# A four-layer graph attention kernel: GpSimd waits in the middle of each pair's gathers for an expansion of scores on TensorE

## The chip, the cores and the metric

The kernel runs on one core of a Trainium2 chip. What is measured is the device time of one execution in microseconds. The engines of the core are TensorE (PE in the profile; PEld is its weight load), VectorE (DVE), ScalarE (ACT), GpSimd (POOL) and SyncE (SP); they run their own instruction streams and are kept in order by counting semaphores, here called counts: an instruction raises a count when it is done, and another engine waits until the count has reached a number.

## What is computed

Four graph attention layers over N = 4096 nodes with 256 features, four heads of 64 (one head in layer 1), each applied to a layer-normed and rectified input and added to the residual. The graph is given as a dense 0/1 matrix `adj` that has some nine neighbours per node. Layer 0, cut to what matters (layers 1 and 2 have the same form with other slopes and ends; layer 3 is scaled dot-product attention over the transposed mask):

```python
h = jnp.maximum(_layernorm(x), 0.0)
Wh = (h @ W).reshape(n, heads, d)
s_i = jnp.einsum('nhd,hd->nh', Wh, a[:, :d])
s_j = jnp.einsum('nhd,hd->nh', Wh, a[:, d:])
e = leaky_relu(s_i[:, None, :] + s_j[None, :, :])
e = jnp.where((adj == 0)[:, :, None], -jnp.inf, e)
alpha = softmax(e, axis=1)
x = x + elu(jnp.einsum('ijh,jhd->ihd', alpha, Wh))
```

## The kernel before

**Sparse work on a dense input.** The kernel reads `adj` once (the first 240 us), turns it into lists of edges, and from then on works edge by edge. A second, dense program in the same kernel is for inputs that don't fit the lists; it doesn't run here. The nodes are cut into T = 32 tiles of 128. Each tile has its edges laid out over KT = 9 columns of 128 partitions, one edge for each partition and column.

**Gathers.** For each tile and column one indirect DMA, issued by GpSimd at L810, fetches the table row of each edge's neighbour (256 features and its score terms) from `tab_d` in DRAM into the buffer `gb`. So a tile has 9 gathers, and a pair of tiles 18. `gb` is a ring: in layers 0 to 2 it has room for RING = 8 tiles. `gp_gather` (L801) waits before tile t for the count `agg` of tile t - 8, that is, until TensorE has summed up the tile whose place is taken; with that it runs four pairs ahead of the arithmetic. At the start of a layer it first waits for the layer's table, then issues the first 8 tiles without a wait. Nothing else is in GpSimd's stream in the layers.

**The groups.** Work goes by groups n = 0 to 16: a group is a pair of tiles (2n, 2n + 1) up to n = 14, and a single tile in the last two. `pe_layer`, `act_layer` and `vec_layer` run one step for each group, in an order that is written out by hand, and the layer that follows (l = L.n + 1) is prepared inside the same steps: as soon as a tile of x is final, its norm, hidden values, projection and table row for the next layer are made.

TensorE's step n (`pe_step`, L1966) is: tile 2n and tile 2n + 1 (`pe_tile`, L1995: nine accumulating matmuls each, shown as 18 records at L1925, count `agg` at the end of each tile); `pe_turn` for group n + 1 (L1901, count `turned_raw`); `pe_hidden`, the transposes of the next layer's hidden values (L1830, count `turned`); the first projection (L1851 and lines after it, count `projected`); `pe_turn_back` (L1909, count `back`); the second projection; in layer 2 also `pe_q` (L1865); and last `pe_expand` for group n + 2 (L1875, 18 matmuls, count `expanded`), which spreads each node's score term over its edges.

VectorE's step n (`vec_step`, L1701) is: multiply the gathered rows of group n by their weights (`vec_weigh`, L1609, six of them, count `weighed`); scores of group n + 1 from the expansion and the gathered terms (`vec_scores`, L1498 to L1518, waits for `expanded`, count `raw_ok`); finish the group's tiles (`vec_finish`, L1620 to L1643); two scans over the scores for the maximum of each node (`vec_shift`, L1554 and L1556, count `shifted`); subtract it (`vec_less`, L1566, waits for `back`, count `lessened`); and statistics and score terms of the next layer.

ScalarE's step (`act_step`, L1076) makes for each tile the matrix that sums edges into nodes (`act_distance` L1008 and `act_equal` L1015, count `S_ok`; L1008 waits for `agg`), scales the outputs (L1047), copies transposes and projections out of PSUM (L926, count `hT_ok`; L948, L959 or L962, count `tabbed`), sends the table rows to DRAM (L966) and exponentiates the scores (`act_exp`, L1024, count `p_ok`).

`expanded` rises by one for each group, 17 in a layer.

Of the kernel before, what the change touches and what calls it, by code (L numbers as in the profile page):

```python
# [445 lines left out]
class Sparse:  # L446
# [354 lines left out]
    def gp_gather(self, e, L, t):  # L801
        gb, s = self.rows(L, t), t % L.ring
        if L.n == 0:
            e.wait_ge(self.listed, t // 4 + 1)
            if t == 6:
                e.wait_ge(self.seg_in, 16 * HS)
        if t >= L.ring:
            e.wait_ge(self.agg, T * L.n + t - L.ring + 1)
        for k in range(KT):
            e.indirect_dma_start(gb[:, 0, k, 0:L.row], None, self.tab_d[L.n],  # L810
                                 bass.IndirectOffsetOnAxis(ap=self.idx[:, t, k:k + 1], axis=0)).then_inc(self.gat[s], 16)
# [1346 lines left out]
```

## Time and profile before

| | us |
|---|---|
| median of 3 runs | 2522.17 |
| lowest and highest of them | 2516.67 and 2530.95 |
| span of the profiled execution | 2533.3 |
| GpSimd busy in it | 1126.0 (44%) |
| VectorE busy in it | 1446.1 (57%) |
| TensorE busy in it | 1404.5 (55%) |
| ScalarE busy in it | 1221.3 (48%) |

The profiled execution is one run of the program under the hardware profiler. Times in the rows below are in us from the span's start. By the gathers, layer 0 goes from 269.9 to about 840, layer 1 to about 1367, layer 2 to about 1914, and layer 3 to the end.

### The profile page before, as it was taken

What the parts mean: (1) busy time and instruction counts of PE and PEld (TensorE: products, weight loads), DVE (VectorE), ACT (ScalarE), POOL (GpSimd) and SP (SyncE); (2) the same over time, 40 slices, a digit from 0 to 9 for tenths busy, and PEclk for the clock granted to TensorE, in tenths of its full rate; (3) what the DMA queues carried; (4) which work ended last, traced back from release to release, by engine and by line L of the source; (5) the groups of instructions that cost most, each with busy time, mean ns of one, the idle gap of its engine ahead of it and who ended that gap; (6) DMA issues with size and microseconds to landing.
All of it is one profiled execution on the core that took longest, in us unless ns stands there. A gap on an engine that the chain in (4) does not pass through costs nothing.

```text
span 2533.3 us, 25363 instructions
## 1 busy us (share of the span) xinstructions
PE 1404.5 (55%) x7265; PEld 1001.1 (40%) x7265; DVE 1446.1 (57%) x4007; ACT 1221.3 (48%) x2974; POOL 1126.0 (44%) x1172
## 2 busy tenths in 40 slices
PE   3564214556657216657674347666694456556655
PEld 2432113444445204445452124444452345444544
DVE  3788656556567315555664145555582566666666
ACT  6775314666667204445563045555582243444344
POOL 0000525666550566656613755555505344455441
PEclk9965556677777656777776567888897677777778
DMA  9993313344430334434412433444415445555451
GB/s 359 388 373 96 75 41 98 105 109 115 99 96 22 93 95 108 112 100 107 108 42 75 106 103 111 111 111 111 110 60 185 119 142 152 148 175 147 143 151 57
DMA packets 163550, 320.34 MB, mean 126 GB/s; under 512 B 31562, under 2 KB 80464, under 8 KB 163408
## 3 DMA queue, kind: packets, MB, share of 16 engines
q0 software_dynamic: 64512, 191.91, 28.3%
q1 hardware_dynamic: 81200, 105.63, 12.6%
q10 hardware_dynamic: 17696, 21.12, 2.4%
q8 instruction: 61, 1.00, 0.2%
q14 instruction: 81, 0.66, 0.1%
HBM read 288.74 MB, written 29.84 MB: 126 GB/s over the span
## 4 chain that ended last, share of the span: by engine, by line
PE 28%; issue 25%; DVE 21%; another core or an unknown queue 16%; ACT 7%; DMA 2%; SPq 1%; ACTq 0%; POOL 0%; DVEq 0%; POOLq 0%
PE ps L1925 17%; PE ps L1851 5%; DVE s_gb L1609 4%; DVE s_sc L1541 2%; ACT s_a L842 2%; DVE s_F L1554 2%; DMA s_adj<-in_adj_dram 2%; PE ps L1889 1%; DVE s_F L1556 1%; DVE s_ST L1417 1%; ACT s_S L1008 1%; PE ps L1865 1%; DVE s_tmp L1537 1%; SPq L642 1%
## 5 line engine op out<-in xcount | busy, mean ns | idle before, releaser
L810 POOL DMA_INDIRECT s_gb<-s_tab,s_ji x1152 | 1121.4, 973 | 1107.1 <-PE ps L1925 368.1
L1925 PE MATMUL ps<-s_gb,s_S 128*128 128x264 f32 (+1 forms) x2304 | 688.5, 457 | 331.3 <-issue 261.1
L1925 PEld LDWEIGHTS ps<-s_gb,s_S 128*128 128x128 f32 x2304 | 523.3, 231 | 480.2 <-issue 318.7
L1008 ACT ACTIVATE s_S<-s_count,s_ji 128x128 f32<-128x128 f32 x1152 | 352.8, 390 | 333.7 <-remote 197.3
L1609 DVE TENSOR_TENSOR s_gb<-s_gb,ps 128x768 f32<-128x768 f32 x384 | 341.7, 948 | 7.7 <-ACT ps L1024 5.9
L1851 PE MATMUL ps<-s_wx,s_hT 128*128 128x264 f32 (+2 forms) x512 | 237.3, 602 | 157.0 <-issue 66.2
L1015 ACT ACTIVATE s_S<-s_S,s_ones 128x384 f32<-128x384 f32 x384 | 209.6, 603 | 86.1 <-remote 67.3
L1851 PEld LDWEIGHTS ps<-s_wx,s_hT 128*128 128x128 f32 x512 | 117.9, 255 | 215.8 <-issue 148.8
L1498 DVE TENSOR_REDUCE s_sx<-ps 128x144 f32<-128x432 f32 (+3 forms) x68 | 30.3, 446 | 245.1 <-remote 242.2
L1889 PE MATMUL ps<-s_early,s_rows_of 128*128 128x256 f32 x416 | 129.9, 466 | 63.1 <-issue 42.9
L1537 DVE TENSOR_TENSOR s_tmp<-ps,s_gb 128x512 f32<-128x512 f32 (+1 forms) x160 | 98.5, 632 | 106.0 <-issue 45.9
L1620 DVE TENSOR_SCALAR s_rc<-ps,s_alone 128x4 f32<-128x4 f32 (+1 forms) x128 | 28.2, 220 | 225.4 <-PE ps L1925 107.8
L1909 PE MATMUL ps<-s_ident,s_F 32*128 32x32 f32 (+3 forms) x272 | 34.1, 246 | 211.0 <-issue 144.3
L1554 DVE TENSOR_TENSOR_SCAN s_F<-s_d,ps 32x512 f32<-32x512 bf16 (+3 forms) x68 | 81.8, 1202 | 113.0 <-remote 64.0
L1889 PEld LDWEIGHTS ps<-s_early,s_rows_of 128*128 128x128 f32 x416 | 95.0, 234 | 83.6 <-issue 45.7
L1024 ACT ACTIVATE ps<-s_sc 128x72 f32<-128x72 f32 (+3 forms) x68 | 15.0, 220 | 231.6 <-DVE s_sc L1567 124.4
L842 ACT ACTIVATE s_a<-s_adj 128x4096 fp8e4<-128x4096 int32 x32 | 115.4, 3606 | 15.6 <-DMA s_adj<-in_adj_dram 15.6
L1909 PEld LDWEIGHTS ps<-s_ident,s_F 32*128 32x128 f32 (+3 forms) x272 | 27.7, 167 | 236.5 <-issue 155.8
L790 POOL IOTA s_u<- 128x1152 f32 x1 | 1.4, 1399 | 236.5 <-DVE s_flag_t L1410 236.5
L1901 PE MATMUL ps<-s_ident,s_sc 128*32 128x128 f32 (+3 forms) x272 | 44.2, 282 | 111.5 <-issue 78.7
L1541 DVE TENSOR_REDUCE s_sc<-s_tmp 128x8 f32<-128x512 f32 (+1 forms) x160 | 97.1, 624 | 0.0
L1566 DVE TENSOR_TENSOR s_sc<-s_sc,ps 128x24 f32<-128x24 f32 (+3 forms) x136 | 23.0, 170 | 128.1 <-remote 99.3
(206 smaller groups left out, 2007.2 us busy)
## 6 DMA issues: line engine op xcount, KB each, us to landing
s_adj<-in_adj_dram SPq DMA_DIRECT2D x32, 2048.0 KB, 16.1
s_gb<-s_tab,s_ji POOLq DMA_INDIRECT x1152
s_mine<-s_tab SPq DMA_DIRECT2D x128, 128.0 KB
s_tab<-s_tb ACTq DMA_DIRECT2D x32, 256.0 KB
s_tab<-s_tb ACTq DMA_DIRECT2D x31, 260.0 KB
s_xs<-in_x_dram SPq DMA_DIRECT2D x8, 512.0 KB, 16.4
s_early<-s_q SPq DMA_DIRECT2D x32, 128.0 KB
s_tab<-s_tb ACTq DMA_DIRECT2D x15, 257.0 KB
```

The costliest lines, as they stand in the source:

```text
L810: e.indirect_dma_start(gb[:, 0, k, 0:L.row], None, self.tab_d[L.n], bass.IndirectOffsetOnAxis(ap=self.idx[:, t, k:k + 1], axis=0)).then_in ...
L842: e.activation(self.a8[:, q % 2], self.adj[:, r], ACT.Copy, saturate=False).then_inc(self.conv)
L1008: m = e.activation(self.s_part(U)[:, i, :], self.count[:], ACT.Square, bias=self.irel[:, t, k:k + 1], scale=-1.0)
L1015: e.activation(self.s_part(U), self.s_part(U), ACT.Relu, bias=self.ones[:, 0:1], scale=-4.0).then_inc(self.S_ok)
L1537: e.tensor_tensor(part(x), self.bank((0, 6, 7)[x % 3]).rearrange("p (k d) -> p k d", k=2)[:, 0:2 if c < 4 else 1], g4[:, 0, 2 * c:min(2 * ...
L1541: e.tensor_reduce(sc[:, 2 * c - 2:min(2 * c, KT), :], part(x - 1).rearrange("p k (h d) -> p k h d", h=4), AX, ALU.add).then_inc(self.dotted)
L1554: e.tensor_tensor_scan(F, d0[:, 0:HE], pc, SEG, ALU.add, ALU.max).then_inc(self.v)
L1609: e.tensor_tensor(vv[:, k], vv[:, k], wide(p[:, k, :], 3, L.hd), ALU.mult).then_inc(self.weighed)
L1851: x = e.matmul(o, self.hT[:, j, k, :], self.wx[:, k, a:b], start=(k == 0), stop=(k == 1 and l < 2))
L1889: m = e.matmul(self.bank((0, 6, 7)[x % 3], D * i, D), self.unfolding(t, k, k + 1), self.q[:, t % 2, :], start=True, stop=True)
L1909: m = e.transpose(pt[:, rows * k:rows * (k + 1)], F[:, P * k:P * k + P], self.ident[0:rows, 0:rows])
L1925: m = e.matmul(o, S[:, i, :], g4[:, 0, k, lo:lo + D + 2 * L.heads], start=(k == 0), stop=(k == KT - 1))
```

## The change

Two lines are added to `gp_gather`. They apply to layers 0 to 2 and to the second tile of each pair that is gathered under the ring's wait, t = 9, 11, ... 29. Before the nine gathers of such a tile GpSimd waits until `expanded` has reached 17 L.n + t // 2 - 1, which is the number it has once the expansion of group t // 2 - 2 is done. The pair that is being gathered is group t // 2. TensorE makes that expansion at the end of step t // 2 - 4, the step in which it also sums tile t - 8.

```diff
         if t >= L.ring:
             e.wait_ge(self.agg, T * L.n + t - L.ring + 1)
+        if L.n < 3 and t >= L.ring and t % 2 and t < 30:
+            e.wait_ge(self.expanded, 17 * L.n + t // 2 - 1)
         for k in range(KT):
             e.indirect_dma_start(gb[:, 0, k, 0:L.row], None, self.tab_d[L.n],
```

Nothing else is changed: the DMAs, their number and their order on the queue are the same, and so are the streams of the other engines.

## Rows read from the trace of the kernel before

**Rows 1.** Page, costliest groups: line, engine, operation, count; busy, mean; idle before, releaser.
```profile
L810 POOL DMA_INDIRECT s_gb<-s_tab,s_ji x1152 | 1121.4, 973 | 1107.1 <-PE ps L1925 368.1
```

**Rows 2.** Windows (columns in the first row): a pair of layer 0, of layer 2, without gathers.
```profile
core 0: us, PE busy (x) PEld busy (x) DVE busy (x) ACT busy (x) POOL busy (x), PEclk, DMA share, GB/s
610.87:637.85 26.98, 16.57 (x75) 12.27 (x74) 16.60 (x47) 17.48 (x50) 17.33 (x19) 0.78 0.43 110
1617.80:1648.65 30.85, 19.77 (x87) 12.86 (x86) 16.45 (x44) 16.23 (x44) 17.27 (x18) 0.83 0.43 113
779.57:800.17 20.60, 15.17 (x66) 11.78 (x65) 16.31 (x48) 17.03 (x49) 0.00 (x0) 0.75 0.04 14
```

**Rows 3.** Timeline, GpSimd: start, length, engine, line [idle before, releaser]; after 18 gathers each.
```profile
637.85 0.94 POOL L810 DMA_INDIRECT s_gb<-s_tab,s_ji  x1 [4.47 <-remote]
...
970.50 0.95 POOL L810 DMA_INDIRECT s_gb<-s_tab,s_ji  x1 [3.28 <-remote]
```

**Rows 4.** Timeline, layer 0, late part of a run of gathers.
```profile
622.25 0.68 PE L1875 MATMUL ps<-s_si,s_ST 128*128 128x24 bf16 x18
...
624.28 6.77 PE L1925 MATMUL ps<-s_gb,s_S 128*128 128x264 f32 x18 [1.35 <-issue]
...
635.33 0.38 PE L1925 MATMUL ps<-s_gb,s_S 128*128 128x264 f32 x1 [1.41 <-issue]
...
636.75 5.22 PE L1925 MATMUL ps<-s_gb,s_S 128*128 128x264 f32 x16 [1.03 <-issue]
636.95 0.61 DVE L1498 TENSOR_REDUCE s_sx<-ps 128x144 f32<-128x432 f32 x1 [8.14 <-remote]
637.13 2.73 ACT L1008 ACTIVATE s_S<-s_count,s_ji 128x128 f32<-128x128 f32 x9 [3.68 <-remote]
```

**Rows 5.** Timeline, layer 0 after its last gather.
```profile
786.39 0.38 DVE L1498 TENSOR_REDUCE s_sx<-ps 128x72 f32<-128x216 f32 x1
```

**Rows 6.** Timeline, layer 0, after the run of gathers that begins at 637.85.
```profile
642.24 0.60 PE L1830 MATMUL ps<-s_ident,s_tb 128*128 128x128 f32 x4
643.09 0.58 ACT L926 ACTIVATE s_hT<-ps 128x512 f32<-128x512 f32 x1
...
645.78 0.43 PE L1909 MATMUL ps<-s_ident,s_F 32*128 32x32 f32 x4 [0.93 <-DVE s_F L1556]
...
647.37 2.06 PE L1851 MATMUL ps<-s_wx,s_hT 128*128 128x258 f32 x4 [1.15 <-ACT s_tb L960]
...
649.22 0.68 PE L1875 MATMUL ps<-s_si,s_ST 128*128 128x24 bf16 x18
...
650.33 0.18 DVE L1566 TENSOR_TENSOR s_sc<-s_sc,ps 128x24 f32<-128x24 f32 x1 [3.37 <-remote]
...
658.84 0.38 ACT L959 ACTIVATE s_tmp<-ps 128x256 f32<-128x256 f32 x1 [4.49 <-remote]
```

**Rows 7.** Timeline, layer 2: an expansion, and the next start of gathers.
```profile
1632.63 0.61 PE L1875 MATMUL ps<-s_si,s_ST 128*128 128x24 bf16 x18
...
1648.65 0.95 POOL L810 DMA_INDIRECT s_gb<-s_tab,s_ji  x1 [8.41 <-PE ps L1925]
```

**Rows 8.** Timeline, layer 1: the first gather after the layer's first 72.
```profile
944.23 0.94 POOL L810 DMA_INDIRECT s_gb<-s_tab,s_ji  x1 [10.71 <-remote]
```

**Rows 9.** Timeline, TensorE in layer 0, beside 27 gathers from 420.1 to 454.9.
```profile
426.74 0.61 PE L1875 MATMUL ps<-s_si,s_ST 128*128 128x24 bf16 x18
430.81 10.24 PE L1925 MATMUL ps<-s_gb,s_S 128*128 128x264 f32 x36 [3.46 <-DVE s_gb L1609]
...
441.32 0.60 PE L1830 MATMUL ps<-s_ident,s_tb 128*128 128x128 f32 x4
459.72 2.09 PE L1851 MATMUL ps<-s_wx,s_hT 128*128 128x258 f32 x4 [17.80 <-ACT s_hT L926]
...
465.21 0.68 PE L1875 MATMUL ps<-s_si,s_ST 128*128 128x24 bf16 x18
```

**Rows 10.** Timeline, GpSimd in layer 1: two run starts, one after the other.
```profile
1078.90 0.95 POOL L810 DMA_INDIRECT s_gb<-s_tab,s_ji  x1 [6.13 <-PE ps L1925]
...
1113.61 0.95 POOL L810 DMA_INDIRECT s_gb<-s_tab,s_ji  x1 [12.20 <-PE ps L1925]
```

## The prediction

> **What bounds the kernel now.** I read four views, in this order. First the groups of instructions: GpSimd's 1152 gathers take 949 to 973 ns each and one starts every 1.25 us [rows 1], so the 18 gathers of a pair (two tiles of 128 nodes) need 22.6 us. Then the windows: a pair of layer 0 takes 27.0 us, one of layer 2 30.9 us, and a pair without any gather beside it 20.6 us [rows 2]. No engine is busy for more than 20 us in any of them. So neither the gathers alone nor the arithmetic alone sets the pair's time; something between them does.
>
> The timeline of GpSimd shows the rhythm: 18 gathers without a break, then a pause of 4.5 or 3.3 us that ends with a count from TensorE (`agg`, the end of the first tile of a pair) [rows 3]. The timeline of the other engines shows the something. TensorE finishes an expansion at 622.9; VectorE, which has nothing else to do for 8.1 us, reads that count only at 636.95, 14.0 us later. TensorE's next tile ends at 631.05, and ScalarE (and GpSimd) act on it at 637.13, 6.1 us later; TensorE itself issues its next matmuls singly, with 1.4 us idle before one, until 636.75 [rows 4]. All of it comes free at once, 3.3 to 3.8 us after the last gather (633.4). Where no gathers run, the same count is there when VectorE comes for it, with no idle time at all [rows 5]. I call the time in which counts are held **the clog**. Counts from TensorE that are raised up to about 7 us into a run of gathers go through (turned 642.84, used 643.09). The `back` raised at 646.2, 8.4 us into the run, is used at 650.3, and the second `projected` (649.4) at 658.8 [rows 6]. So a run of 18 gathers has a clog from about +8 to +26 us, counted from its first gather.
>
> What matters is therefore **what lies in the clog**. Now a run starts when tile A of a pair is summed (in the rows: expansion 622.25, tile A 624.28, run 637.85). Tile B (4 us) and the chain that goes back and forth between TensorE and the others (transposes, `turned`, hT, projection, row, second projection, expansion, at +12.1 us) lie in the clear part. The clogged part holds the next tile A, a stream of 18 matmuls that needs few counts. That is a good alignment.
>
> **The change, part by part.** It removes nothing and adds 33 waits (odd tiles 9 to 29, three layers). No DMA, no arithmetic. The wait itself is an instruction of some 20 to 50 ns on GpSimd; 33 of them I cost at nothing. What is queued behind it on GpSimd is the pair's second 9 gathers and all later ones; who waits for those is VectorE's scores, six tiles later, so a late gather costs nothing directly. SP's and ScalarE's queues are passed by nothing. What changes is when the gathers run, and so where the clog falls.
>
> Step 1, the first pause. The first 9 gathers end at +11.3 us. The expansion waited for is finished at +12.1 (637.85 to 649.9) in layer 0 and at +15.4 in layer 2 (1617.8 to 1633.2) [rows 6, 7]. The clog after 9 gathers must first drain. No row shows such a drain alone: 18 gathers have pauses of 3.3 to 4.5 us and 72 of them 10.7 us [rows 3, 8], 0.12 to 0.14 us for each gather, so 9 have 2 to 3 us, of which 0.7 us is GpSimd's own restart; below by the 0.8 us of the expansion itself. I take 2.3, near the rows with the short pauses. The second half then starts at about +13.6 (layer 0) or +16.1 (layer 2).
>
> Step 2, whether there is a second pause. Tile A of the next pair starts 1.4 to 2 us after the expansion and takes 6.8 us [rows 4], so its count is raised 7 to 8 us after the second half began: at the very edge where counts still go through. The second half ends only at +11.3 after its start. If the count is in by then, GpSimd goes on without a pause, and its run of 18 now starts at the expansion, not at the end of tile A.
>
> Step 3, what that does. From the expansion, tiles A and B take 10.2 us [rows 9] and their transposes end near +13, deep in the clog of the run. The chain can then not go on before the run ends and drains: 0.7 + 22.6 + 3.6 = 26.9 us, and from `turned` to the end of the expansion it takes 7.1 us (642.84 to 649.9) [rows 6]. A pair takes 34.0 us. And GpSimd waits for that same expansion, so the next run starts there again: the bad alignment keeps itself. The trace of before has it once, where 27 gathers ran without a stop: TensorE was through with both tiles and transposes at 441.9 and got its next work at 459.7, 17.8 us idle, and from expansion to expansion went 38.5 us [rows 9]. A second case is in layer 1, where tile B came late in its run: 34.7 us for that pair [rows 10].
>
> The sum, against 2533.3 us of the profiled execution. Layer 0: 34.0 - 27.0 = 7.0 us a pair. Layer 2: its chain is 3.3 us longer (+15.4 against +12.1), so 37.3 - 30.9 = 6.4. Layer 1: about 33 (its chain is a little shorter than layer 0's; the row with 34.7 bounds it from above, the present 28.6, five runs from 970.50 to 1113.61, from below), so 4.4 [rows 2, 3, 10]. Each layer has 11 such pairs. The bad alignment starts at once in layer 0 (the expansion that tile 11 will wait for ends at 465.9, 6 us after its gathers start now [rows 9]), but tile A's count is at the edge, so some pairs get a second pause instead and cost nothing. I take 8 pairs of 11 in layers 0 and 2, where tile A follows the expansion at once, and 3 of 11 in layer 1, where it follows later and so misses the edge more often: 8 x 7.0 + 3 x 4.4 + 8 x 6.4 = 120 us. 2533 + 120 = 2653 for a profiled execution. The median of the runs is 0.4% under the profiled one (2522.17 to 2533.3), so **2640 us**. With all 33 pairs: 77 + 48 + 70 = 195 us, 2717. Layer 3 and the first 380 us have no such wait and stay.
>
> **The rivals.** (a) *Two pauses a pair, faster.* If tile A's count is just late, more than 8 us into the second half, each half of 9 gathers gets its own drain and the clog is cut from 18 us a pair to about 2 x 5. A pair is then 2 x (11.3 + 2.3) = 27.2 us, the same as layer 0 has, 1.4 less than layer 1, and in layer 2, where the present pause of 8.4 us [rows 7] shows TensorE itself held by the clog, the expansion at 15.4 + 0.7 and then 13.6 make 29.7, 1.2 less: -15 - 13 = -28 us, 2494. With a drain of 2.6 us it is -10. For it: the clog is the only reason why a pair takes 27 and not 20.6, and this halves it. Against it: 1 us decides, and a long wait for an expansion always lands on the wrong side. It would be visible in pairs of 27 with two pauses each. If even more of layer 2's excess goes (to the 26.5 us at which one drained run of 18 can repeat) the sum is -70, 2452. (b) *The wait does nothing.* Should the count of the expansion be there at +12.1, GpSimd loses 1 us in the middle and has a shorter pause at the end, which is 3.3 us or more everywhere: 2522. The held count [rows 4] speaks against it. (c) *All pairs bad*, 2717, the end of my forecast's own case.
>
> The Trainium skill speaks for (b): "Advanced Engine Details and Errata", section DMA Bandwidth Details, puts the overhead of a semaphore increment on TRN2 at about one cycle. By that rule the expansion's count would be seen when it is raised, no run of gathers could hold it, and the change would give 2522. The 14.0 us in the trace disagrees, and where both differ the trace decides.
>
> **How the numbers follow.** Forecast, run realigned to the expansion: 0.63, of which most lies in 2570 to 2720. Rival (a): 0.25, 2450 to 2510. Rival (b), or gains and losses that cancel: 0.12. A measurement of this kernel can tell about 0.5% (13 us) from no change. So faster 0.25, same 0.12, slower 0.63. The range has to reach (a) and the case of all pairs bad: 2490 to 2725 leaves out about 0.2. The forecast's own range is 2570 to 2725.
>
> **What would show it.** Right: in the changed kernel GpSimd pauses 8 to 11 us in the middle of a pair and not between pairs, from expansion to expansion goes 33 to 37 us, and TensorE sits idle some 12 us before the first projection of a pair, waiting for hT. Step 1 alone is right if the first 9 gathers are followed by 2 to 3 us. Step 2 is wrong if a pair has two pauses of 2 to 3 us each; then (a) holds. Step 3 is wrong if the pause is in the middle only and the pair still takes 27: counts would then pass through the clog that I take for held. If VectorE reads the expansion's count without idle time and nothing else moves, it is (b). The prediction fails above all if tile A's count comes 1 us later than I reckon.

## The result, and the profile after

The changed kernel takes **2712.81 us** (median of 4 runs, 2701.56 to 2719.67), the kernel before 2523.2: a ratio of **1.073** (95% interval 1.068 to 1.078). The profiled execution spans 2705.1 us, 171.8 more than before. Forecast were 2640 us and a slower kernel; 2713 is nearly the upper end of the forecast's own case, which had all pairs bad at 2717.

The page, four of the costliest groups (columns as in [rows 1]). GpSimd now stands idle before gathers 185 us longer in all, and the expansion (L1877) ends 355 us of its idle time. TensorE's projection (L1853) waits 492 us for hT, which ScalarE copies at L928; before it was 98 us. ScalarE's copy itself waits 475 us, and VectorE's first step on a summed tile (L1622) 489 us, for a count whose source the profile can't name (remote):

```profile
L812 POOL DMA_INDIRECT s_gb<-s_tab,s_ji x1152 | 1108.6, 962 | 1292.0 <-PE ps L1877 354.8
...
L1853 PE MATMUL ps<-s_wx,s_hT 128*128 128x264 f32 (+2 forms) x512 | 281.0, 697 | 565.3 <-ACT s_hT L928 492.1
...
L1622 DVE TENSOR_SCALAR s_rc<-ps,s_alone 128x4 f32<-128x4 f32 (+1 forms) x128 | 28.0, 219 | 565.8 <-remote 488.9
L928 ACT ACTIVATE s_hT<-ps 128x512 f32<-128x512 f32 (+1 forms) x67 | 38.4, 573 | 500.2 <-remote 475.3
```

Windows of one pair of layers 0, 1 and 2, each from one resumed run of gathers to the next. They answer [rows 2]; the work per pair is the same, only the time is longer. The clock granted to TensorE is lower (0.65 for 0.78 in layer 0), but it is busy only 0.6 us longer in the pair (17.17 for 16.57), so the clock does not explain the 6 us:

```profile
core 0: us, PE busy (x) PEld busy (x) DVE busy (x) ACT busy (x) POOL busy (x), PEclk, DMA share, GB/s
625.70:659.00 33.30, 17.17 (x74) 13.11 (x74) 16.70 (x47) 17.45 (x50) 17.26 (x18) 0.65 0.34 90
1105.80:1140.50 34.70, 17.85 (x79) 13.14 (x79) 15.80 (x49) 14.04 (x36) 17.02 (x18) 0.65 0.32 87
1695.60:1733.00 37.40, 18.82 (x88) 12.00 (x87) 16.58 (x45) 16.50 (x45) 16.99 (x18) 0.77 0.33 94
```

GpSimd's timeline, layer 0. The pauses of 10.8 to 11 us are in the middle of a pair (they answer [rows 3]); between pairs, at 603.83, the idle time is 0.43 us, hardly more than the 0.3 before any gather:

```profile
603.83 0.94 POOL L812 DMA_INDIRECT s_gb<-s_tab,s_ji  x1 [0.43 <-issue]
...
625.73 1.21 POOL L812 DMA_INDIRECT s_gb<-s_tab,s_ji  x1 [10.95 <-PE ps L1877]
...
659.00 0.94 POOL L812 DMA_INDIRECT s_gb<-s_tab,s_ji  x1 [10.84 <-PE ps L1877]
```

TensorE and then, in the last line, ScalarE in the pair between those pauses:

```profile
624.27 0.68 PE L1877 MATMUL ps<-s_si,s_ST 128*128 128x24 bf16 x18
628.06 11.05 PE L1927 MATMUL ps<-s_gb,s_S 128*128 128x264 f32 x36 [3.12 <-DVE s_gb L1611]
...
639.39 0.60 PE L1832 MATMUL ps<-s_ident,s_tb 128*128 128x128 f32 x4
652.04 2.09 PE L1853 MATMUL ps<-s_wx,s_hT 128*128 128x258 f32 x4 [12.05 <-ACT s_hT L928]
...
657.54 0.68 PE L1877 MATMUL ps<-s_si,s_ST 128*128 128x24 bf16 x18
...
651.39 0.60 ACT L928 ACTIVATE s_hT<-ps 128x512 f32<-128x512 f32 x1 [10.53 <-remote]
```

The expansion ends at 624.95 and the 18 gathers run from 625.7 to 648.1. Both tiles and their transposes are through at 640. ScalarE sees the transposes' count at 651.39, 11.4 us after it was raised and 3.3 us after the last gather; then come 7 us of chain, and the expansion, finished at 658.2, lets GpSimd go on. That is the loop of step 3.

That the second nine gathers of a pair come later is not itself the cost. VectorE waits for gathered rows as long as before, 37.5 us in all and in two places (here its line among the waits: total, times, longest); before it was 37.6:

```profile
DVE s_sc L1508 <- DMA s_gb<-s_tab,s_ji: 37.5, 2, 19.8
```

Where the time went: the time from a layer's third expansion to its sixteenth (ends of L1875 or L1877 in TensorE's timeline) is 353, 362 and 389 us in layers 0 to 2 of before and 402, 423 and 460 of after, +50, +61 and +71. The starts of layers are within 1 us of what they were, and layer 3 is 10 us shorter.

### The profile page after: what moved, and what is told of

Read it like the earlier page. It is cut to its first block, busy times and chain, and to the rows that moved or that the text cites. A ratio compares the mean times of both kernels' runs of the same rounds, so it can differ in the third digit from the quotient of the medians.

```text
span 2705.1 us, 25385 instructions
## 1 busy us (share of the span) xinstructions
PE 1391.5 (51%) x7265; PEld 996.5 (37%) x7265; DVE 1444.9 (53%) x4007; ACT 1220.3 (45%) x2974; POOL 1113.2 (41%) x1172
## 4 chain that ended last, share of the span: by engine, by line
another core or an unknown queue 29%; DVE 23%; PE 18%; issue 15%; ACT 10%; DMA 2%; SPq 1%; ACTq 0%; DVEq 0%
PE ps L1927 8%; PE ps L1853 6%; DVE s_gb L1611 5%; ACT s_S L1010 3%; DVE s_sc L1543 2%; DVE s_F L1556 2%; ACT s_a L844 2%; DMA s_adj<-in_adj_dram 1%; DVE s_F L1558 1%; PE ps L1867 1%; SPq L642 1%; DVE s_ST L1419 1%; DVE s_tmp L1539 1%; PE ps L1891 1%
## 5 line engine op out<-in xcount | busy, mean ns | idle before, releaser
L812 POOL DMA_INDIRECT s_gb<-s_tab,s_ji x1152 | 1108.6, 962 | 1292.0 <-PE ps L1877 354.8
L1927 PE MATMUL ps<-s_gb,s_S 128*128 128x264 f32 (+1 forms) x2304 | 619.5, 431 | 136.8 <-issue 76.7
L1927 PEld LDWEIGHTS ps<-s_gb,s_S 128*128 128x128 f32 x2304 | 490.9, 216 | 246.3 <-issue 91.9
L1853 PE MATMUL ps<-s_wx,s_hT 128*128 128x264 f32 (+2 forms) x512 | 281.0, 697 | 565.3 <-ACT s_hT L928 492.1
L1853 PEld LDWEIGHTS ps<-s_wx,s_hT 128*128 128x128 f32 x512 | 136.6, 295 | 634.3 <-ACT s_hT L928 503.9
L1622 DVE TENSOR_SCALAR s_rc<-ps,s_alone 128x4 f32<-128x4 f32 (+1 forms) x128 | 28.0, 219 | 565.8 <-remote 488.9
L928 ACT ACTIVATE s_hT<-ps 128x512 f32<-128x512 f32 (+1 forms) x67 | 38.4, 573 | 500.2 <-remote 475.3
L1911 PEld LDWEIGHTS ps<-s_ident,s_F 32*128 32x128 f32 (+3 forms) x272 | 33.7, 194 | 212.0 <-issue 141.8
L1049 ACT ACTIVATE s_y<-ps,s_rc 128x64 f32<-128x64 f32 x384 | 87.1, 307 | 4.7 <-DVE ps L1645 4.6
```

Source lines behind the costliest of these rows:

```text
L1049: m = e.activation(y[:, L.hd * h:L.hd * h + L.hd], ov[:, L.hd * h:L.hd * h + L.hd], ACT.Copy, scale=self.rc[:, j, h:h + 1])
L1853: x = e.matmul(o, self.hT[:, j, k, :], self.wx[:, k, a:b], start=(k == 0), stop=(k == 1 and l < 2))
L1927: m = e.matmul(o, S[:, i, :], g4[:, 0, k, lo:lo + D + 2 * L.heads], start=(k == 0), stop=(k == KT - 1))
```

## Experiments

Theory, **held counts**: while gathers follow closely, counts that TensorE raises are held till a backlog is served, and the change costs only because it moves the chain into that stretch. The spacing is the time from the start of one gather to the start of the next. Main rivals: the late gathers or the wait cost by themselves; any gather in flight holds counts, at whatever spacing.

The kernel before was run beside each experiment. In four sessions it took 2505 to 2549 us, as in the session of the result (2523); in two others it took 2006 and 2007 us. The traces from sessions of the first kind show held counts, except those of experiment 5, whose session is known only by the time of the kernel before (2507 us) and by the sign given in the last section. The traces from the other two show none. I call these sessions **held** and **free**. Chips differ between sessions, but one chip number stands for sessions of both kinds, so whether it is the chip, its host or something that changes with time stays open. Ratios are only compared within a session.

**1. The wait on an older expansion, and three more kernels: a free session.** First the wait alone (the diff is against the changed kernel):

```
-            e.wait_ge(self.expanded, 17 * L.n + t // 2 - 1)
+            e.wait_ge(self.expanded, 17 * L.n + t // 2 - 2)
```

> The same 33 waits in the same places, but each for the expansion one pair earlier, which was done some 27 us before. If what costs is the phase between the gathers and TensorE's chain (my theory, the held counts), nothing happens: no pause in mid-pair, 27.0 us per pair in layer 0, 2517 to 2531 us, ratio 1.00. If the waiting instruction itself, or its place in GpSimd's queue, cost something (rival), 33 of them would carry part of the 190 us, and the time would be above 2540 us.

Measured: 2010.8 us, ratio 1.001 (0.9995 to 1.003). The same as before, but so was everything that ran beside it. Next, the changed kernel with a run of gathers that starts at tile B (again against the changed kernel):

```
         if t >= L.ring:
-            e.wait_ge(self.agg, T * L.n + t - L.ring + 1)
+            e.wait_ge(self.agg, T * L.n + t - L.ring + (2 if L.n < 3 and t % 2 == 0 and t < 30 else 1))
```

> The changed kernel with one more edit: the first nine gathers of a pair are started one tile later (at the end of tile B, not of tile A). The wait of the change stays, and all gathers come later than in the changed kernel by their own waits. Theory of the held counts: the run starts 7.7 us after the expansion, the next expansion is made 8 us into the run (layer 0) or 11 (layer 2), so that at worst a pause of 2.3 us after nine gathers is added to one of 3.3: 26 to 28 us per pair in layer 0, at most 31 in layer 2, 2440 to 2540 us. Rival (late rows: it costs that the second nine gathers wait at all, and that VectorE gets their rows later): nothing gets better than in the changed kernel, 2700 us or more.

Measured: 2009.2 us, ratio 1.001 (0.999 to 1.003). The last two have one memset after each gather, without and with the waits of the change:

```
         self.idle = sb("idle", [P, 32])
...
+            if T * L.n + t + k:
+                e.wait_ge(self.idled, KT * (T * L.n + t) + k)
+            e.memset(self.idle[:], 0.0).then_inc(self.idled)
```

> The kernel before with a small GpSimd memset (128x32, result unused) after each gather and no new wait. It should bring the spacing of the gathers from 1.25 us to about 1.43 (0.13 for the memset and some 0.05 for its issue). Theory: counts are held because gathers are issued faster than about one in 1.40 us, which is how fast a backlog of 18 and of 72 was seen to drain. Then no count is held: 18 gathers take 25.8 us, VectorE reads TensorE's counts within 0.1 us in mid-run, a pair takes 26 to 27.5 us in all three layers (now 27.0, 28.6, 30.9), and the kernel takes 2400 to 2470 us although GpSimd does more. Rival (any gather in flight holds counts, at whatever spacing): each pair is 3 us longer, 29 to 30 us in layer 0, 2580 us or more.

Measured: 2012.2 us, ratio 1.002 (1.000 to 1.004). The spacing did not rise to 1.43 us but to 1.26: the memset fits into the 0.3 us between two gathers.

> The changed kernel (with its 33 waits) with the same memset after each gather. Theory: with no held counts the expansion waited for is finished at about the end of the first nine gathers (12.9 us at the new spacing) and is seen at once, so the wait costs 0 to 2 us a pair: within 60 us of the kernel with the memset alone, and below 2530 us. Rival (the wait costs because rows come late, whatever the counts do): 170 to 190 us above the kernel with the memset alone, with a pause in mid-pair of 10 us or more.

Measured: 2010.4 us, ratio 1.001 (0.999 to 1.003), against 2012.2 without the waits. So the 33 waits alone cost nothing in a free session, where they are always met before GpSimd comes to them (see below): the cost that I gave the instruction is right.

The trace of the first of the four shows what a session without held counts looks like. Here are two lines of its page: GpSimd's group among the costliest, and the gathers among the DMA issues, where the last number is the time to landing in us:

```profile
L812 POOL DMA_INDIRECT s_gb<-s_tab,s_ji x1152 | 1132.4, 983 | 572.9 <-issue 344.2
...
s_gb<-s_tab,s_ji POOLq DMA_INDIRECT x1152, 3.3
```

A window from the end of one expansion of layer 0 to that of the next (columns as above):

```profile
493.16:513.80 20.64, 15.40 (x75) 12.04 (x74) 16.80 (x50) 17.15 (x49) 15.88 (x16) 0.75 0.48 133
```

TensorE's timeline, the first projection in that window:

```profile
507.62 1.14 PE L1853 MATMUL ps<-s_wx,s_hT 128*128 128x258 f32 x4 [1.42 <-ACT s_hT L928]
```

GpSimd goes on for 200 us without a pause at the same 1.25 us spacing, and yet TensorE stands idle for hT only 1.42 us, against 12.05 in the changed kernel's held trace. The pair takes 20.6 us, as long as a pair without gathers in [rows 2]. So closely spaced gathers are not enough to hold counts: how fast counts are served is not the same everywhere. Here the expansion that the change waits for is finished 4 us (the first in layer 0) to 49 us (the first in layer 2) before GpSimd comes to the place of the wait.

**2. The changed kernel again: a held session.**

> The changed kernel itself, on the chip on which the four runs before it were made. There the kernel before takes 2007 us instead of 2523 and its trace shows no held counts (18 gathers follow on 18 with 0.3 us between, and a pair of layer 0 takes 20.4 us). Theory of the held counts: what the change costs, it costs only through them; without them the expansion waited for was finished some 50 us before, and the changed kernel takes 2000 to 2020 us, ratio 1.00. Rival (the change costs by itself, on any chip): a ratio of about 1.07, 2150 us.

Measured: 2719.9 us against 2524.5, ratio 1.076 (1.071 to 1.082). The session turned out to be a held one, so this repeats the result (pairs of 33.3, 34.7 and 37.4 us) and says nothing of the changed kernel without held counts; what does is the changed kernel with one memset per gather above (2010 us).

**3. One memset after each gather, held session.** The same kernel as the third above.

> The kernel before with a 128x32 GpSimd memset after each gather, again, for a chip on which counts are held (where the kernel before takes 2524 us). The first run of it, on the chip without held counts, showed what the memset does to the spacing: 1.43 us. Theory (counts are held while gathers are issued faster than one in 1.40 us): no count is held at 1.43, a pair takes 26 to 27.5 us in all three layers, 2400 to 2470 us or less, down to the 2012 us of the other chip. Rival (any gather in flight holds counts on this chip, at whatever spacing): pairs 3 us longer, 2580 us or more. Should it land on the chip without held counts: 2012 us again, ratio 1.00.

Measured: 2466.4 against 2504.5 us, ratio 0.985 (0.980 to 0.990), spacing 1.26. There is more work on GpSimd, and yet the kernel is 1.5% faster. In its trace 44 us are gained before the third expansion of layer 0 ends (383 us for 427 in the trace of the kernel before, which is of another session); why stays open. It does not test the rate, since 1.26 us is below 1.40. The pairs take 26.4, 27.0 and 28.9 us on average, 0.7 to 1.0 less than in the kernel before.

**4. Two memsets (spacing 1.30 us), without and with the waits of the change, held session.**

```
+            if T * L.n + t + k:
+                e.wait_ge(self.idled, 2 * (KT * (T * L.n + t) + k))
+            for j in range(2):
+                e.memset(self.idle[:, j, :], 0.0).then_inc(self.idled)
```

> The kernel before with two GpSimd memsets (128x24 each, results unused) after each gather, no new wait. One memset had left the spacing at 1.26 us (it fitted into the 0.3 us gap), so it tested nothing; two should bring it to 1.45 to 1.50. Where counts are held (before at about 2520 us): theory (each gather brings counts that the chip serves at 1.40 us per gather, first in, first out): at 1.47 us nothing piles up, VectorE reads TensorE's expansion within 1 us in mid-run, a pair takes 26.5 to 28 us in all three layers (before 27.0, 28.6, 30.9), 2300 to 2430 us. Rival (gathers in flight hold counts at any spacing): a pair takes 18 x 1.47 + 3.5 = 30 us in layer 0, 2600 us or more. On the chip without held counts (before at 2007): GpSimd's gathers become the bound, 26.5 us instead of 22.6 per pair, 2080 to 2200 us.

> The changed kernel with the same two memsets after each gather. Theory: with nothing held, the 33 waits find their expansion finished or nearly so (its count comes 12 us after the run's start in layer 0, the first nine gathers take 13.2), 0 to 3 us a pair: at most 60 us over the kernel with the memsets alone. Rival (the wait costs by itself, because the second nine gathers come late): 170 to 200 us over it, with pauses of 10 us or more in mid-pair.

Measured: 2477.9 us without the waits (ratio 0.972, 0.970 to 0.975) and 2690.8 with them (1.056, 1.053 to 1.058). The spacing was 1.30, not 1.47, since memsets that don't wait for each other take 0.19 us together. So counts were still held, and the change cost 213 us (190 at 1.25). The timelines of GpSimd, first without and then with the waits:

```profile
550.88 0.95 POOL L811 DMA_INDIRECT s_gb<-s_tab,s_ji  x1 [2.97 <-remote]
...
578.03 0.95 POOL L811 DMA_INDIRECT s_gb<-s_tab,s_ji  x1 [3.00 <-remote]
```

```profile
593.99 1.21 POOL L813 DMA_INDIRECT s_gb<-s_tab,s_ji  x1 [9.06 <-PE ps L1882]
...
627.68 0.95 POOL L813 DMA_INDIRECT s_gb<-s_tab,s_ji  x1 [9.74 <-PE ps L1882]
```

Both expectations missed, and these rows show why. In layer 0 the pair stays about as long: 27.1 us for 27.0, and 33.7 against 33.3 with the waits. The 18 spacings take 0.9 us more of it (23.4 for 22.5), so that what is left beyond them is shorter: 3.7 for 4.5 us, and 10.3 for 10.8. A backlog served at 1.40 us a gather would do just that: 18 of them are through 25.2 us after the first, whether they were issued in 22.5 or 23.4. But this rests on layer 0 alone. In layers 1 and 2 the pairs are 1.0 us longer than in the kernel before (the table below), as the rival has it; the two traces are from different sessions, so the rows don't decide.

Nor does the rate say how long a count is held in the middle of a run. If counts were served in their turn among the gathers, a backlog that grows by 0.15 us with each gather could hold one that TensorE raises after ten or twelve gathers for some 2 us (an estimate). In [rows 4] VectorE reads one 14.0 us late, and in the changed kernel ScalarE acts 11.4 us late, when all 18 gathers are through. So the order in which counts are served is open.

**5. Two memsets, each waited for (spacing 1.54 us), without and with the waits of the change, held session.**

```
             e.indirect_dma_start(...).then_inc(self.gat[s], 16)
+            for j in range(2):
+                e.memset(self.idle[:], 0.0).then_inc(self.idled)
+                e.wait_ge(self.idled, 2 * (KT * (T * L.n + t) + k) + j + 1)
```

> The kernel before with two memsets (128x28) after each gather, each waited for before GpSimd goes on. Two memsets that follow on each other without a wait had taken 0.19 us together and left the spacing at 1.30; waited for, they should take 0.35 to 0.5, and the spacing be 1.45 to 1.60 us, above the 1.40 at which a backlog of counts was seen to drain. Theory: now, for the first time, nothing piles up: on a chip that holds counts TensorE's expansion is read within 1 us in mid-run, E to E is the larger of 18 spacings (26 to 29 us) and some 21 to 25 of chain, in all three layers, the first tiles of a layer gain most (60 to 77 us between its first expansions become 40 or less), and the kernel takes 2250 to 2420 us where before takes about 2520. Rival (gathers in flight hold counts at any spacing): 18 x 1.5 + 3.5 = 30.5 us per pair in layer 0, 2600 us or more. On a chip that holds nothing (before at 2007): 2080 to 2250 us, bound by GpSimd.

> The changed kernel with the same two memsets and waits after each gather. Theory: what the change costs, it costs through held counts; with none, the expansion it waits for is finished at about the end of the first nine gathers (12.1 us after the run's start against 13.5), the pause in mid-pair is 0 to 3 us, and the kernel is within 60 us of the paced kernel without the wait. Rival (the wait costs by itself, or spacing does not matter): 150 to 220 us over it, with pauses of 9 us or more in mid-pair, as at a spacing of 1.30 us (2691 against 2478 us).

Measured: 2295.7 us without the waits (ratio **0.915**, 0.912 to 0.917, against 2507.3) and **2292.0** with them (0.914, 0.911 to 0.916). The same 33 waits that cost 190 to 213 us at 1.25 and 1.30 cost nothing at 1.54. Here are two lines from the page of the kernel without them, its chain of waits by engine and its group of gathers:

```profile
POOL 59%; issue 20%; PE 8%; ACT 5%; DVE 5%; DMA 2%; SPq 1%; ACTq 0%; POOLq 0%; DVEq 0%
...
L811 POOL DMA_INDIRECT s_gb<-s_tab,s_ji x1152 | 1134.8, 985 | 509.0 <-POOL s_idle L814 320.5
```

Its window of a pair of layer 0, and then TensorE's timeline in the pair after it:

```profile
554.00:582.70 28.70, 17.37 (x74) 12.86 (x73) 15.74 (x46) 16.85 (x49) 22.11 (x55) 0.68 0.39 103
```

```profile
604.28 2.09 PE L1855 MATMUL ps<-s_wx,s_hT 128*128 128x258 f32 x4 [3.47 <-ACT s_hT L930]
```

An expansion in its layer 2, and VectorE's first step on it, beside unbroken gathers:

```profile
1452.08 0.61 PE L1879 MATMUL ps<-s_si,s_ST 128*128 128x24 bf16 x18
...
1453.16 0.61 DVE L1502 TENSOR_REDUCE s_sx<-ps 128x144 f32<-128x432 f32 x1 [0.27 <-PE ps L1879]
```

GpSimd bounds this kernel (59% of the chain), not a held count: 18 x 1.54 = 27.7 us and a little more at each tile make a pair of 29 in all three layers, once the first pairs of layer 0 are past. The wait for hT is 3.5 us, beside unbroken gathers, and ScalarE makes hT as soon as its work before it is done. VectorE uses the expansion's count 0.5 us after the expansion's end, where [rows 4] have 14.0. With the waits, GpSimd stands idle 0.67 us before a gather behind a wait, against 0.61 before the same gather without it (timeline of GpSimd, paced and changed):

```profile
608.01 0.95 POOL L813 DMA_INDIRECT s_gb<-s_tab,s_ji  x1 [0.67 <-PE ps L1881]
```

The expectation had the awaited expansion finish at about the end of the first nine gathers. It is finished 52 to 63 us before GpSimd comes to the wait, nearly everywhere, since GpSimd is now the slower one. So these waits are met long before, and the run shows that they cost nothing then; it does not show what the phase does without held counts.

The gain is not in the pairs, which are as long as in the kernel before or a little longer, but where many gathers stand in a row. Times in us, each from the end of one expansion to that of another in TensorE's timeline (first: the third of layer 0; pairs: a layer's third to sixteenth; starts: from there to the next layer's third; layer 3: its third to its last):

| kernel | spacing | first expansions end at | pairs of layers 0, 1, 2 | starts of layers 1, 2, 3 | layer 3 |
|---|---|---|---|---|---|
| before, held | 1.25 | 427 | 353, 362, 389 | 171, 162, 156 | 472 |
| changed, held | 1.25 | 426 | 402, 423, 460 | 171, 162, 157 | 462 |
| two memsets, held | 1.30 | 396 | 350, 375, 402 | 155, 144, 149 | 465 |
| paced, held | 1.54 | 369 | 358, 380, 388 | 128, 121, 121 | 391 |
| paced and changed, held | 1.54 | 368 | 356, 380, 384 | 127, 121, 121 | 390 |
| one memset, free | 1.26 | 370 | 267, 304, 312 | 118, 111, 114 | 381 |

Paced at 1.54, a held session's starts and layer 3 come within 10 us of a free one's. Whether that is the spacing itself or that GpSimd waits for counts of its own was not taken apart; both keep the gathers from running ahead.

**6. The changed kernel with a later start, and a pace of 1.44 us: a free session.** The diff of the first is the second one of experiment 1; the other is the kernel before with three memsets after each gather that don't wait for each other and one wait for the last.

> The changed kernel with one more edit: a pair's first nine gathers wait for the end of tile B four pairs back, not of tile A, so they start later still by their own waits. The 33 waits of the change stay. On a chip that holds counts. Theory (only the phase between the run of gathers and TensorE's chain matters): tile B ends some 12.7 us after the expansion; the next expansion is made 8 us into the run in layer 0 and 11.4 in layer 2, so at worst the backlog of nine gathers (9 x 1.40 = 12.6, then 1 us) stands before it: two pauses of about 2 and 1 to 3 us instead of one of 11 to 15, 26 to 29 us per pair in layer 0 (changed kernel 33.3), at most 32 in layer 2 (37.4), 2440 to 2560 us: two waits are faster than one. Rival (gathers that come later cost by coming later): slower than the changed kernel, 2720 us or more. On a chip that holds nothing it takes 2009 us, as measured before.

> The kernel before, paced at 1.47 us per gather instead of 1.54: three memsets (128x16) after each gather that don't wait for each other (0.25 us together) and one wait for the last (0.27). At 1.54 GpSimd was the bound: 29 us per pair, 2296 us. Theory: 1.47 is still above 1.40, so nothing is held, and some 45 pairs each lose 1.3 us: 2220 to 2260 us. Rival (the limit lies between 1.47 and 1.54, since the other DMAs and engines raise counts too): held counts come back, pairs of 30 us or more in layers 1 and 2, 2300 to 2450 us.

Measured: 2005.7 us (1.000, 0.9985 to 1.002) and 2173.2 us (1.081, 1.077 to 1.086), against 2006.1. The session was free, so neither question was answered: the phase alone and where between 1.30 and 1.54 the holding ends stay open. What the second does show is the price of pacing where nothing is held, 167 us. Two lines of its page, as in experiment 1:

```profile
L811 POOL DMA_INDIRECT s_gb<-s_tab,s_ji x1152 | 1131.4, 982 | 494.4 <-POOL s_idle L814 305.1
...
s_gb<-s_tab,s_ji POOLq DMA_INDIRECT x1152, 2.8
```

So none of these kernels is the fastest in both kinds of session. Paced at 1.54 wins 8.5% in held sessions; the pace of 1.44 loses 8.1% in a free one, where the kernel before is the fastest.

## Why the prediction was right, and where its number was off

- **What bounds the kernel** (counts held by runs of gathers): right, and the experiments bear it out. Spread the gathers to 1.54 us, and the wait for hT, the layer starts and the change's cost shrink together. What the prediction could not know from one trace is that the holding is not a property of the kernel alone; in a free session it is gone, and so is any effect of the change (2010 us with the waits, 2012 without).
- **The wait instruction at nothing**: right, but shown in free and paced runs only. In the paced ones a gather behind it starts 0.03 to 0.06 us later.
- **Step 1, a first pause of 2.3 us**: seen only in the first pairs of a layer (2.1 and 2.4 us, for tile 9 of layer 1 and tile 11 of layer 0); afterwards the pause is that of the loop. The working had a slip: less the restart of 0.7 us, pauses of 3.3 to 4.5 us after 18 gathers are 0.14 to 0.21 us for each gather, not 0.12 to 0.14.
- **Step 2, tile A's count at the edge**: this is where the number failed. I took counts to go through up to 7 or 8 us into the second half, so that some pairs would miss it. In the changed kernel's trace tile A ends up to 10.2 us after the expansion, 9.4 us into the second half, and GpSimd still goes on, with 0.3 us idle, or 0.43 at 603.83. Behind a pause in mid-pair the longest pause before the next pair is 1.9 us. One reason is that GpSimd doesn't look for this count before its nine gathers are issued, 11.3 us into the half, so a count raised at 9 us can come 2 us late and cost nothing. Why it isn't held for 4 us like the `back` of [rows 6], raised at 8.4 us, is open; the pause before the half is 11 us here and was 4.5 us there.
- **Step 3, the loop**: right in mechanism and size. Forecast 34.0, about 33 and 37.3 us per pair; measured 33.3, 34.7 and 37.4, with pauses of 11, 12.5 and 15.2 us and TensorE 12.05 us idle before its projection.
- **The sum**: the mis-sized term is layer 1. I took 3 pairs of 11 at 4.4 us, 13 us, because tile A would follow its expansion later there and miss the edge. It follows at once, since all it needs has long been ready while TensorE waited, and it ends only 5.6 to 7.5 us after the expansion. So 9 of 11 pairs pause 10 us or more, at 34.7 - 27.8 = 6.9 us each, 62 us. (27.8 is 362 us by 13 pairs; the 28.6 that I had from five run starts was too long.) Layer 2 has 9 bad pairs instead of 8, and each gained more than 6.4 us, since the pairs before took 29.9 us on average and not 30.9: +71 against 51. Layer 0 has the 8 bad pairs that I took, 50 us against 56. That 8 and 9 came out near my 8 is luck: I had counted off pairs in which tile A would miss the edge, and only one did, the last of layer 0. The others that stay shorter are a layer's first, with the waits of tiles 9 and 11. In all it is 182 us against 120, less 10 in layer 3. The trace of experiment 2 has the 182 again (50, 64 and 68 us by layer), but layer 3 there is only 4 us shorter than in the kernel before, so the 10 us vary from run to run and can't be put down to the change.
- **Rival (a), two pauses**: did not occur beyond a layer's first pairs. In layer 0 tiles 10 and 11 have pauses of 3.4 and 2.4 us, in layer 2 of 3.1 and 4.6, and then the loop takes over. Behind a bad pair pauses of over 1 us between pairs are there twice, late in layer 0 (1.2 and 1.9 us), and the first of them saves nothing: 10.3 us follow in mid-pair, and the pair takes 33.4. After the second 4.7 us follow, hT comes 8 us late and not 11, and the pair takes 29.2 us: a pair at the edge that saves 4 us against the loop, but not a pair of 27 with two short pauses. The trace of experiment 2 has this pair too.
- **Rival (b), the wait does nothing**: false where counts are held, and true in a free session. The Trainium skill ("Advanced Engine Details and Errata", DMA Bandwidth Details) puts the overhead of a semaphore increment on TRN2 at about one cycle. The free sessions don't contradict that: TensorE has hT after 1.42 us of idle time there. The held ones do: ScalarE uses the count for hT 11.4 us after it was raised.
- **Rival (c), all pairs bad, 2717**: the time came out within 5 us of it, but that is luck, since 26 of 33 pairs were bad, with those of layers 1 and 2 dearer than reckoned.
- That the **phase** is what matters (the run begins at the expansion, not at tile A) rests on the traces: the loop is there in every late pair. The run that should have undone it fell into a free session, so this is argued from the order of events in the traces and no run tests it.

## What to carry to other kernels

A wait costs little by its own length; look at what the engine issues behind it, and at what else happens while that runs. A chain that goes back and forth between engines needs its counts promptly. Where counts are held, as here in the held sessions, it should not lie beside the densest stretch of small DMAs, and a wait that ties the start of that stretch to the end of the chain can lock the two in the worst phase. Run the kernel before again in other sessions before tuning to a stall of a few us that no instruction explains: here the stall, worth a fifth of the time, was not there in all of them.

## What the hardware showed that I had not expected

- The same kernel takes 2505 to 2549 us in some sessions and 2006 in others, and I found no other difference in the work that the traces record. A sign in the profile's page tells them apart: in the held ones, experiment 5 among them, it has no time to landing for the transfers of table rows (`s_mine<-s_tab` and `s_tab<-s_tb`), and in the free ones it has (2.3 to 3.6 us). For the gathers it has one in four of the six free traces only, 2.8 to 3.3 us.
- In a held session counts raised in the middle of a run of gathers come through 3.3 to 3.8 us after the last of 18 gathers at a spacing of 1.25 us, and at 1.54 nothing is held. That the backlog is served at one gather in about 1.40 us is an estimate, from TensorE's single issues 1.4 us apart [rows 4] and pauses of 3.3 and 10.7 us after 18 and 72 gathers; it fits the pairs of layer 0 at 1.25 and 1.30 us, and not how long a count is held in mid-run.
- A GpSimd memset of 128x32 after each gather costs 0.01 us of spacing. Two that wait for each other cost 0.29.
- Spreading the gathers by 23% made the kernel 8.5% faster in a held session, and by 15% made it 8.1% slower in a free one.
